# Two-layer graph kernel: attention logits taken from the feature matmul and spread by DMA, two exponentials a head

## The reference

```python
h = max(layernorm(x), 0)                              # layer 0
feats  = einsum('bnf,hfu->bhnu', h, W)
dense  = e_self[..., :, None] + e_neigh[..., None, :] # e_* = feats . a_self, feats . a_neigh
dense  = leaky_relu(dense, 0.2) + NEG_BIG * (1 - A)
out    = einsum('bhij,bhju->bhiu', softmax(dense), feats) + b
x = x + relu(out)
h = max(layernorm(x), 0)                              # layer 1
h = relu(Dn * H @ (Be * H^T @ (h @ W1^T)) + b1);  h = layer_norm(h) * gamma + beta
x = x + Dn * H @ (Be * H^T @ (h @ W2^T)) + b2 + h_in
```

## Time and profile before

| what | value |
|---|---|
| median of three runs | 2789.54 us (2789.48 to 2792.99) |
| the profiled execution's own time | 2788.78 us |
| its span, first to last instruction | 2786.9 us |
| TensorE clock granted, mean | 0.997 |
| PE, PEld busy | 98%, 81% |
| DVE, ACT, POOL busy | 81%, 50%, 51% |
| DMA | 33 GB/s over the span |

### The profile page before, as it was taken

One profiled execution on the slowest core, in us unless ns is written; L12 is line 12 of the kernel. 1 busy time (PEld: TensorE's weight loads), 2 busy tenths in 40 slices (PEclk: granted clock), 3 DMA queues, 4 the chain that ended last, 5 costly groups with the idle time before them and its releaser, 6 DMA issues.

```text
span 2786.9 us, 48329 instructions
## 1 busy us (share of the span) xinstructions
PE 2730.4 (98%) x14740; PEld 2249.7 (81%) x14740; DVE 2270.0 (81%) x4259; ACT 1390.4 (50%) x2955; POOL 1410.0 (51%) x2462
## 2 busy tenths in 40 slices
PE   5999999999999999999999999999999999999998
PEld 3888888888888888888888888888888888888886
DVE  8888887888788888878887888888788878888885
ACT  4545554554555455545545554555455455545553
POOL 6455455545554554555455545545554555455453
PEclk9999999999999999999999999999999999999999
DMA  3000010010001000100100010001001000100000
GB/s 127 29 29 28 32 34 28 28 38 28 28 28 38 28 28 31 35 28 28 37 29 28 28 38 28 28 31 35 28 28 37 29 28 28 38 28 28 31 31 16
DMA packets 58967, 91.01 MB, mean 33 GB/s; under 512 B 6592, under 2 KB 22976, under 8 KB 58944
## 3 DMA queue, kind: packets, MB, share of 16 engines
q1 hardware_dynamic: 58944, 90.74, 10.0%
HBM read 57.16 MB, written 33.55 MB: 33 GB/s over the span
## 4 chain that ended last, share of the span: by engine, by line
DVE 32%; PE 32%; POOL 16%; issue 15%; ACT 5%; POOLq 0%; DVEq 0%; DMA 0%; SPq 0%; ACTq 0%
POOL z_lo L408 6%; DVE x L753 5%; POOL rest L392 4%; PE p_w1b L820 3%; PE p_w1b L818 3%; PE p_w1b L819 3%; DVE att L620 3%; DVE r L685 2%; PE p_w1a L818 2%; PE p_w1a L819 2%; PE p_w1a L820 2%; DVE st L756 2%; DVE st L696 2%; PE p_att L896 2%; DVE feats L668 2%
## 5 line engine op out<-in xcount | busy, mean ns | idle before, releaser
L321 POOL TENSOR_TENSOR ve<-mv,eps 128x1 f32<-128x1 f32 x384 | 75.3, 196 | 991.9 <-DVE mv L689 676.5
L441 ACT ACTIVATE att<-att,neg_max 128x128 f32<-128x128 f32 x1024 | 325.9, 389 | 334.3 <-DVE neg_max L624 334.3
L818 PE MATMUL p_w1a<-W_hi,rT_hi 128*128 128x512 f32 x1024 | 416.2, 406 | 0.0
L819 PE MATMUL p_w1a<-W_lo,rT_hi 128*128 128x512 f32 x1024 | 405.7, 396 | 0.0
L820 PE MATMUL p_w1a<-W_hi,rT_lo 128*128 128x512 f32 x1024 | 404.9, 395 | 0.0
L518 ACT ACTIVATE h<-x,nb,rs 128x512 f32<-128x512 f32 x128 | 104.5, 816 | 580.7 <-POOL nb L333 580.7
L620 DVE TENSOR_TENSOR att<-att,mask 128x512 f32<-128x512 f32 x256 | 309.8, 1252 | 0.0
L408 POOL TENSOR_TENSOR z_lo<-z,z_hi 128x512 fp32r<-128x512 f32 x128 | 231.7, 1810 | 115.3 <-ACT z_hi L546 115.3
L780 DVE SCALAR_TENSOR_TENSOR z<-p_w1a,rs,t_bc 128x512 f32<-128x512 f32 x128 | 96.1, 751 | 232.0 <-PE p_w1a L820 232.0
L365 POOL TENSOR_TENSOR en_rhs<-en_parts,head_rows 32x1024 fp32r<-32x1024 f32 x128 | 241.9, 1890 | 37.0 <-POOL rs L327 35.2
L896 PEld LDWEIGHTS p_att<-feats,attT 128*128 128x128 f32 x2048 | 248.2, 192 | 13.2 <-ACT attT L474 1.4
(11 more groups left out here) (129 smaller groups left out, 6952.0 us busy)
## 6 DMA issues: line engine op xcount, KB each, us to landing
x_in<-in_x SPq DMA_DIRECT2D x128, 256.0 KB, 2.8
out<-raw SPq DMA_DIRECT2D x128, 256.0 KB, 2.1
adj_in<-in_adj SPq DMA_DIRECT2D x128, 128.0 KB, 2.6
raw<-in_W1T SPq DMA_DIRECT2D x2, 1024.0 KB, 11.0
raw<-in_W2T SPq DMA_DIRECT2D x2, 1024.0 KB, 9.8
raw<-in_W0T SPq DMA_DIRECT2D x1, 1024.0 KB, 6.3
b_bc<-in_b SPq DMA_DIRECT2D x2, 256.0 KB, 9.5
b_bc<-in_b SPq DMA_DIRECT2D x1, 512.0 KB, 9.2
```

The costliest lines, as they stand in the source:

```text
L441: last = nc.scalar.activation(att[:, i, :], att[:, i, :], ACT.Exp, bias=neg_max[:, i:i + 1])
L818: mm(dst, hi, w_hi, start=first, stop=False)
L819: mm(dst, hi, w_lo, start=False, stop=False)
```

## The change

The 16 vectors that give the logits (8 for e_neigh, 8 for e_self) become 16 more columns of W0. The feature matmul is written as two halves, p_fa (256 feature columns and 16 logit columns) and p_fb (256 columns). The logits thus come out with nodes on partitions. DVE copies them to `e_blk`, transposes the 32x32 blocks of e_blk to `eT`, SP writes the neighbour logits by four DMAs to a small buffer in device memory (`en_rows`), waits for them, and loads it back by one DMA of 512 KB into all partitions (`u`). POOL adds the mask (0 or -2^36) to u. DVE takes the row maximum of u, and from it and the self logit the maximum of the leaky score. Leaky relu is the larger of s and 0.2 s, and the exponential rises with its argument, so ACT takes two exponentials a head (scale 1 and scale 0.2, each with its own shift), and DVE takes the larger (`larger`). The matmuls for p_e and for the scores, the split of the logits, en_rhs and the three 1024-element DVE steps of the scores go away.

The order changes too. AHEAD becomes 4, so features are made for graph t+3 and the first norm for t+4. PE runs both halves of hidden, then the transposes of r half a, then G x z of t-1. ACT takes the exponentials of the second four heads of t+1 at the start of a turn, and those of the first four heads of t+2 after rT_hi half b and G_hi and before h of t+1. POOL does the mask and u of t+2 first, then rs2, then the first norm's rstd, then the second's. Core of the diff:

```diff
-        W0_hi, W0_lo = (sb(n, [P, DC, D], F32R) for n in ("W0_hi", "W0_lo"))
-        Wa = sb("Wa", [P, DC, P], F32R)
+        W0_hi, W0_lo = (sb(n, [P, DC, 2, D2 + EW], F32R) for n in ("W0_hi", "W0_lo"))
...
+        p_fa = bank("p_fa")
+        p_fb = bank("p_fb")
+        p_G = p_tb[:, 0:N + 1]
...
# SP, turn
+                g = t.plus(4)
+                if g.within(NG) and (g.loop is not None or g.base >= 4):
+                    load(g)
+                g = t.plus(2)
+                if g.within(NG):
+                    sp.wait_ge(s_eT, g.count())
+                    for q in range(4):
+                        sp.dma_start(en_rows[:, 32 * q:32 * (q + 1)], eT[32 * q:32 * q + HEADS, :]).then_inc(s_en_out, 16)
+                    sp.wait_ge(s_en_out, g.count(per=64))
+                    sp.dma_start(u[:, g.slot(2), :, :].rearrange("p h n -> p (h n)"),
+                                 en_rows.rearrange("(a h) n -> a (h n)", a=1).broadcast_to([P, HEADS * N])).then_inc(s_en_bc, 16)
...
# POOL, turn
+                    pool.wait_ge(s_mask, g.count())
+                    pool.wait_ge(s_en_bc, g.count(per=16))
+                    nc.gpsimd.tensor_tensor(u[:, g.slot(2), :, :], u[:, g.slot(2), :, :],
+                                            mask[:, :].unsqueeze(1).broadcast_to([P, HEADS, N]), ALU.add).then_inc(s_u, 1)
+                g = t
+                if g.within(NG):
+                    rstd(g, mv2, ve2, rs2, s_mv2, s_ve2, s_rs2, s_z)
+                g = t.plus(4)
                 if g.within(NG):
                     rstd(g, mv0, ve0, rs0, s_mv0, s_ve0, s_rs0, s_xn, nm0, s_nm0)
                     shift(g, nm0, rs0, nb0, s_nm0, s_rs0, s_nb0)
...
# ACT
             def exps(g, half):
-                act.wait_ge(s_max, g.count(per=2) - 1 + half)
+                act.wait_ge(s_shifts, g.count())
+                if g.has(1):
+                    act.wait_ge(s_attT, g.count(1))
+                    act.wait_ge(s_att, g.count(1, per=2))
                 for i in range(half * HH, (half + 1) * HH):
-                    last = nc.scalar.activation(att[:, i, :], att[:, i, :], ACT.Exp, bias=neg_max[:, i:i + 1])
+                    nc.scalar.activation(att[:, i, :], u[:, g.slot(2), i, :], ACT.Exp, bias=shifts[:, 0, i:i + 1])
+                    last = nc.scalar.activation(att_low[:, i, :], u[:, g.slot(2), i, :], ACT.Exp, bias=shifts[:, 1, i:i + 1],
+                                                scale=SLOPE)
                 last.then_inc(s_exp, 1)
...
+                    act.wait_ge(s_rT, g.count(per=2))
+                    nc.scalar.activation(rT_hi[:, HALF:DH], p_tb[:, :], ACT.Copy).then_inc(s_rT_hi, 1)
                     if g.has(1):
                         act.wait_ge(s_y, g.count(1))
                     nc.scalar.activation(G_hi[:, :], G[:, g.slot(4), 0:N], ACT.Copy).then_inc(s_G_hi, 1)
+                if t.plus(2).within(NG):
+                    exps(t.plus(2), 0)
...
# DVE
+            def larger(g, half):
+                dve.wait_ge(s_exp, g.count(per=2) - 1 + half)
+                heads = slice(half * HH, (half + 1) * HH)
+                nc.vector.tensor_tensor(att[:, heads, :], att[:, heads, :], att_low[:, heads, :], ALU.max).then_inc(s_att, 1)
...
+                    dve.wait_ge(s_u, g.count())
+                    nc.vector.reduce_max(neg_max[:, :], u[:, g.slot(2), :, :], X, negate=True).then_inc(s_max, 1)
...
+                if t.plus(2).within(NG):
+                    larger(t.plus(2), 0)
                 g = t
                 if g.within(NG):
                     dve.wait_ge(s_w2, g.count())
...
# PE
-            def features(c):
-                return three(p_f[:, :], h0[:, c, 0, :], h0[:, c, 1, :], W0_hi[:, c, :], W0_lo[:, c, :], c == 0, c == DC - 1)
+            def features(c, b):
+                dst, n = ((p_fa, D2 + EW), (p_fb, D2))[b]
+                return three(dst[:, 0:n], h0[:, c, 0, :], h0[:, c, 1, :], W0_hi[:, c, b, 0:n], W0_lo[:, c, b, 0:n], c == 0, c == DC - 1)
```

More of the change, by code:

```diff
@@ L11 @@
 P = 128
-AHEAD = 3
+AHEAD = 4
 UNROLL = 4
@@ L15 @@
 SLOPE = 0.2
-NEG_BIG = -1e10
+ABSENT = -float(2 ** 36)
 TINY = 1e-30
@@ L521, in turn @@
                         rounded(3)
+                g = t
+                if g.within(NG):
+                    act.wait_ge(s_z, g.count())
+                    if g.has(1):
+                        act.wait_ge(s_y, g.count(1))
+                    nc.scalar.activation(z_hi[:, :], z[:, :], ACT.Copy).then_inc(s_z_hi, 1)
+                g = t.plus(1)
+                if g.within(NG):
                     act.wait_ge(s_hg, g.count())
@@ L528, in turn @@
                 if g.within(NG):
-                    for b in range(2):
-                        act.wait_ge(s_scores, g.count(per=2) - 1 + b)
-                        if b == 0 and g.has(1):
-                            act.wait_ge(s_attT, g.count(1))
-                        nc.scalar.activation(att[:, b * HH:(b + 1) * HH, :].rearrange("p h n -> p (h n)"),
-                                             p_att[:, b * HALF:(b + 1) * HALF], ACT.Copy, scale=SLOPE).then_inc(s_sloped, 1)
                     act.wait_ge(s_G, g.count())
@@ L634, in turn @@
                                                    b1_bc[:, 0:HALF], ALU.mult, ALU.add).then_inc(s_pre, 1)
-                g = t.plus(2)
+                if t.plus(1).within(NG):
+                    larger(t.plus(1), 1)
+                g = t.plus(3)
                 if g.within(NG):
@@ L741, in turn @@
                                             ALU.mult).then_inc(s_osc, 1)
-                if t.plus(2).within(NG + 1):
-                    dve.wait_ge(s_cnt1, t.plus(2).count())
-                    nc.vector.reciprocal(inv0[:, :], cnt[:, :]).then_inc(s_inv0, 1)
                 if t.within(NG):
@@ L844, in turn @@
                     hidden(g, 0, p_w1a)
+                    hidden(g, 1, p_w1b)
+                    pe.wait_ge(s_r, g.count(per=2) - 1)
+                    if g.plus(3).within(NG):
+                        pe.wait_ge(s_h0_lo, g.plus(3).count())
+                    transposes(p_ta, r[:, 0:HALF], s_rT)
                 g = t.plus(-1)
@@ L869, in turn @@
                     last.then_inc(s_attT, 1)
[L870 removed]
+                g = t.plus(3)
                 if g.within(NG):
                     pe.wait_ge(s_h0_lo, g.count())
[L874 to L881 removed]
                     if g.base == 0:
                         pe.wait_ge(k_lo0, 1)
+                        pe.wait_ge(k_wa_lo, 2)
                     if g.has(1):
[L887 to L889 removed]
+                        pe.wait_ge(s_feats_sb, g.count(1, per=2))
+                    for c in range(2):
+                        features(c, 0)
+                        features(c, 1)
                 g = t.plus(1)
@@ L917, in turn @@
                     last.then_inc(s_w2, 1)
-                if t.plus(2).within(NG):
-                    features(DC - 2)
+                g = t.plus(3)
+                if g.within(NG):
+                    features(2, 0)
                 g = t.plus(1)
@@ L930, in turn @@
                     last.then_inc(s_hg, 1)
+                g = t.plus(3)
+                if g.within(NG):
+                    features(2, 1)
+                    features(3, 0)
+                    features(3, 1).then_inc(s_feats, 1)
                 g = t.plus(2)
                 if g.within(NG):
-                    features(DC - 1).then_inc(s_feats, 1)
-                    pe.wait_ge(s_en_rhs, g.count())
-                    pe.wait_ge(s_es_lhs, g.count())
-                    if g.has(1):
-                        pe.wait_ge(s_osc, g.count(1))
-                    for b in range(2):
-                        dst = p_att[:, b * HALF:(b + 1) * HALF]
-                        last = mm(dst, es_lhs[:, :], en_rhs[:, b * HH:(b + 1) * HH, :].rearrange("p h n -> p (h n)"),
-                                  start=True, stop=True)
-                        last.then_inc(s_scores, 1)
                     pe.wait_ge(s_beT, g.count())
                     pe.wait_ge(s_row, g.count())
+                    if t.base == -1:
+                        pe.wait_ge(k_mean_sb, 2)
                     if g.has(1):
```

322 lines of the change are left out of this document (123 added, 199 removed).

## The result

The changed kernel takes 2811.97 us (median of four runs, 2808.87 to 2813.74), the kernel before 2790.22. The ratio is 1.0075, with a 95% interval of 1.0062 to 1.0088: slower by 22 us. The forecast was 2823, slower.

The account below looks back on a forecast made before the run. Two loops of 21.3 us a turn were taken to bound the kernel: PE's, and one through mv1 and h. 2788.8 + 126 x (21.5 - 21.28) + 6 = 2822.5, with the median 0.8 above: 2823; range 2745 to 2865.

Parts of the forecast that it names:

- PE after the change: PE's own work per turn, with logits and scores removed and features narrowed: from 21.28 us to 19.95, say 20.0.
- The other loop, step by step: Path from hidden through mv2, POOL, xn, rT_hi, rT_lo, x1, mv1, h and hg: the turn closes at 21.0 us.
- The port: Two-SBUF-input `larger` on DVE delays POOL's rs or nb behind mv1 each turn: 0.4 to 0.5 us.
- The further 0.1 for the three small DVE instructions beside rs0: Three small two-input DVE instructions falling on POOL's rs0 add 0.1 us a turn, bounds 0 and 0.3.
- The fill: AHEAD = 4 adds a turn before turn 0, with round trip and u in the path: +6 us, bounds 0 and +14.
- No collision: Rival: `larger` misses POOL's small instructions or barely holds them; turn 21.0, time 2760; 0.29 including a slight collision.
- PE as the bound: Rival: xn in front of rT_hi costs nothing and x1 comes 0.9 sooner; turn 20.0, time 2634; chance 0.04.
- The late round trip: Rival: u lands after 7.8, not 6.8, so POOL delays rs2 and rs0; at 8.5, time 2912; chance 0.10.

Follow-up runs that it names:

- the two best kernels: The changed kernel with ACT's xn behind rT_hi half b and G_hi, alone (2628.12 us) or with DVE's `larger` also behind z (2628.25 us).
- run 2755: The changed kernel with `larger` for the first four heads behind z (2755.45 us), or in place but one column a head (2755.01 us).
- run 2628: The changed kernel with ACT's xn behind rT_hi half b and G_hi (2628.12 us), or with `larger` also behind z (2628.25 us).
- Both moves: The changed kernel with DVE's `larger` for the first four heads behind z and ACT's xn behind rT_hi half b and G_hi: 2628.25 us.
- Two extra trips: The changed kernel with two more 1 KB writes to device memory, each waited for, before u is loaded: 2950.36 us.

## Why the prediction was right

*PE after the change.* The removed and added work had the stated size: 0.12 for 256 columns and 0.125 for 272. The floor of 20.0 is what the two best kernels run at (19.94). The saving of 0.9 us of PE work was real, and none of it arrived, because the other loop held the turn at 21.4: six more matmuls cost next to nothing in the changed kernel, and with that loop shortened the saving arrives. That the two loops were of equal length in the kernel before is read from its rows; no run tried it.

*The other loop, step by step.* In parts of a turn, from the first hidden matmul, forecast and measured: r half b 5.91 and 5.86, mv2 10.1 and 10.09, xn 12.45 and 12.41, rT_hi 13.2 and 13.13, rT_lo 13.8 and 13.74, x1 14.4 and 14.35, mv1 15.9 and 15.97. That is within 0.1 throughout. DVE shed 295 us, and that went into waits for rT_hi, for PE's halves and for hg_hi.

*The port.* `larger` held POOL by 0.47, within the stated 0.4 to 0.5. It was nm that was held and not rs, since `larger` came at 0.31 behind mv1 and not at 0.55. The exponentials end 2.44 after the first of them starts and not 2.58, and mv1 comes 0.1 later on that clock. There is luck in this. Without a hold rs begins 0.54 behind mv1, and nb 1.23. A `larger` at 0.55 would begin just behind rs and end as nb begins, and with xn moved, where it comes at 0.65, it holds neither. So at its own offset the collision may well have cost nothing, by these starts; no run has that offset. The size came right, the way there only in part.

*What was off.* The further 0.1 for the three small DVE instructions beside rs0 was not there: mv2 to xn took 1410.68 - 1408.36 = 2.32, to the hundredth the sum of its steps in the kernel before. The turn in the middle was thus 21.41 and not 21.5, and with the short turns at the end 21.37: 16 us less over 126 turns. Three smaller things go the other way. The fill cost 8.6 and not 6, the end 0.7 and not 0, and the median lies 3.1 over the profiled execution and not 0.8. Together that is the difference of 11 between 2823 and 2812. The loop's pass round, 0.09 in every fourth turn before, is gone too: the turns in the middle of the changed kernel differ by 0.04 at most; that a wait swallows it is my reading. Why the fill is longer is open. POOL's u of graph 0 starts at 35.0, of graph 1 at 48.6, and it takes 4.47 there, in place of 2.4. And the clock granted to TensorE in the fill was at its lower level (0.50, 1.2 GHz) for 20.5 us in three stretches, where it was so for 13.7 us in two before.

*The rivals.* No collision was put at 2760, and the kernels without it, `larger` moved or short, run 2755. PE as the bound was put at 2634, and the kernels without either cause run 2628. So the prices of both were right, and their conditions were one edit away. The late round trip did not come: POOL began on u at 6.6 into the turn (forecast 6.8).

*The expectations that missed.* With xn moved I expected part of the collision to stay (2685 to 2745; 2628 measured). By the windows it should have. Both moves came out 12 us under their range, since PE's own turn was put at 20.0 to 20.1 and is 19.93. The six matmuls in the kernel with xn moved were to cost 93 us and cost 77, by what was still lost before hg. Two extra trips came out in their range, but through `cnt`, which the expectation doesn't have.

## What to carry to other kernels

Where a second loop is as long as the one that is shortened, work taken out gives nothing; follow the other through every engine before counting the saving. Where an in-order engine has an instruction that waits for a slow chain in front of one that is ready, as xn before rT_hi, the swap can be worth more than the change itself: here the same change is slower by 0.75%, and faster by 5.8% with one instruction moved. And a VectorE instruction with two SBUF inputs belongs where GpSimd has nothing on the critical path, even if GpSimd's work there is one column wide: here one such place was worth 57 us.

## What the runs showed of the hardware

In these runs a one-column GpSimd instruction that begins well inside the two-input `larger` is held until 0.05 after its end: nm in the changed kernel (0.66), ve with rs0 first (0.61), nb with xn moved and six more matmuls (0.52), each 0.19 otherwise. An nb that began 0.11 before its end took 0.19. An rs of 0.55 that began 0.11 before `larger` neither held it (0.69, as alone) nor was held. The Trainium skill (SBUF — State Buffer, "Who interferes with whom") says that whoever issues first has the shared ports for the whole instruction. The runs agree for long instructions (rest at 1.70; with both moves `larger` begins inside rest and takes 1.46), and not for this one: by the rule `larger` would have waited 0.44 for rs to end. The measurement decides. That rs reads only at its beginning is my reading of it and was not tried by itself.

A one-input VectorE instruction can be held as well. The scaling of 8 columns of e_blk, which reads and writes SBUF, takes 1.14 beside POOL's z_lo in the changed kernel, and ends when z_lo does:

```profile
1420.29 1.14 DVE L599 TENSOR_SCALAR e_blk<-e_blk 128x8 f32<-128x8 f32 x1
```

```profile
1420.11 1.29 POOL L389 TENSOR_TENSOR z_lo<-z,z_hi 128x512 fp32r<-128x512 f32 x1
```

With `larger` moved behind z it begins 0.20 before z_lo and takes 0.27. DVE had time there, so it cost nothing. With two extra trips it did cost: `cnt`, of two columns, takes 1.2 and not 0.14 beside POOL's u.

The way through device memory is short: a load issued behind a wait starts 1.17 after the last of the small writes, and its 512 KB land in 3.5 (the page's median).

```profile
1399.80 0.26 SPq L269 DMA_DIRECT2D en_rows<-eT  x1
1400.97 0.34 SPq L271 DMA_DIRECT2D u<-en_rows  x1
```
